# A recommender's interaction and MLP on one core: the first loads without waits, more of the weights turned among chunk 0's products, and chunk 0's grams made whole by three accumulated products

## The chip, the core and the metric

The kernel runs on one core of a Trainium2 chip. Its engines are TensorE (PE; its weight loads, PEld, overlap its products), VectorE (DVE), ScalarE (ACT), GpSimd (POOL) and SyncE (SP), which here issues all DMAs on one queue. Each engine runs its own instructions in order and waits on semaphores for the others. The metric is the device time of one execution in microseconds; the median of several executions is given. All times below are in microseconds unless marked ns.

## What is computed

2048 samples, each with 27 feature vectors of 128 numbers and one more vector of 128 (the bottom MLP's output). For each sample all dot products between its features are made, the 351 below the diagonal are joined to the bottom vector and a zero, and these 480 numbers go through four layers with ReLU and one last product.

```python
dots = jnp.einsum('bfd,bgd->bfg', bottom_output, bottom_output)   # 27 x 27 per sample
pairs = dots[:, _TRIL_I, _TRIL_J]                                 # 351
x = jnp.concatenate([bottom_mlp_output, pairs, pad], axis=1)      # 480
for w, b in ((w0, b0), (w1, b1), (w2, b2), (w3, b3)):             # 1024, 1024, 512, 256
    x = jax.nn.relu(x @ w.T + b)
return x @ w_out.T + b_out
```

## The kernel before

**Numbers in halves.** Products run in a 4-byte form of reduced precision (`F32R`). To keep full precision each operand is split into a high half, which the form holds exactly, and the rest, the low half; a product is then three: high by high, high by low, low by high. ScalarE makes the high half by a copy, VectorE the low one by a subtraction.

**Chunks.** The 2048 samples are 8 chunks of 256. A chunk's products stand with the samples as the 256 moving columns: layer 0 has 8 output tiles of 4 inner tiles, layer 1 has 8 of 8, layer 2 has 4 of 8, layer 3 has 2 of 4, each times three products: 96, 192, 96 and 24. Each output tile (a "slot") fills one of two accumulator banks; ScalarE drains it with ReLU (L654) and VectorE splits it (L772, L774).

**Units.** While chunk c's products run, chunk c+1's features are turned into grams in 16 units of 16 samples. A unit is: a load of 108 rows (4 samples of 27 features) by 4 groups (`load_rows`, L344), 4 transposes (`turn`, L502), a high and a low half (L624, L736), 4 gram products of 256 columns (`gram`, L518), which make high by high and high by low beside each other, 4 copies of the diagonal blocks (`gram_parts`, L641), and on VectorE a transpose of the high by low block and two sums (L751, L753, L763), since low by high is the transpose of high by low. A gram comes `XT_LAG` = 2 units after its turn. The finished grams are spilled to memory (L355) and the pairs gathered from there in another layout (L366); ScalarE and VectorE split the pairs (L664, L806), and the next chunk can begin.

**The written order.** Every engine walks the same list of steps. For chunk c, `chunk_steps` writes the products in order and, after every `HOOK` = 9 of them in layers 0 and 1, one hook: the next unit's steps, or in chunk 0 first the weight groups that are left:

```python
if layer < 2 and done % HOOK == 0:
    hook()
```

**Weights.** They arrive with outputs in the partitions and must be turned. A weight group is 4 transposes of 128 columns (L472, L485), a high half (L609, L610, L613) and a low half (L723, L725, L729); there are 34 and one small one for the biases. GpSimd first puts W0's columns in the kernel's own pair order (L444). Groups can be turned in the head, before chunk 0: eight of W1 between the units of chunk 0, then W0, the small one, W3 and W2; the other eight of W1 are turned in chunk 0's hooks.

**The head.** Chunk 0's own units have no products to hide behind. SyncE issues its 16 feature loads into a ring of 4 buffers, each waiting for the buffer's turn, and weight loads in between:

```python
for u in range(ROWS_RING, 8):
    load_rows(0, u)
load_weights(stage_b[:, 0:2, :], w1, 0, 2, w1_head_loaded[0])
```

Then come the spill and the gather of chunk 0, and its first products. Chunk 7 has no units. The functions that the change touches:

Of the kernel before, what the change touches and what calls it, by code (L numbers as in the profile page):

```python
# [5 lines left out]
F32 = mybir.dt.float32  # L6
F32R = mybir.dt.float32r
ALU = mybir.AluOpType
# [31 lines left out]
W1_HEAD, W0_ALL, SMALL = list(range(9, 17)), list(range(W0_GROUPS)), [W0_GROUPS]  # L40
W1_TAIL, W2_ALL, W3_ALL = list(range(17, 25)), list(range(25, 33)), list(range(33, 35))
ORDER = W1_HEAD + W0_ALL + SMALL + W3_ALL + W2_ALL + W1_TAIL
BETWEEN_UNITS, FIRST_BETWEEN = 8, 7
BEFORE_CHUNK = W_GROUPS - len(W1_TAIL)
W0_TURNED = ORDER.index(W0_ALL[-1]) + 1
assert W0_TURNED >= BETWEEN_UNITS

# [16 lines left out]
HOOK = 9  # L64

OUT_UNIT = 2
# [71 lines left out]
def first_steps():  # L138

    steps = []
    for u in range(UNITS + XT_LAG):
        steps += unit_steps(u)
        if 0 <= u - FIRST_BETWEEN < BETWEEN_UNITS:
            steps.append(("weights", u - FIRST_BETWEEN))
    steps += [("weights", n) for n in range(BETWEEN_UNITS, W0_TURNED)] + [("mlp",)]
    return steps + [("weights", n) for n in range(W0_TURNED, BEFORE_CHUNK)] + [("pairs",)]

def chunk_steps(gram, weights=False):  # L150

    steps, done, unit, group = [], 0, 0, BEFORE_CHUNK if weights else W_GROUPS

    def hook():
        nonlocal unit, group
        if group < W_GROUPS:
            steps.append(("weights", group))
            group += 1  # L160
        elif gram and unit < UNITS + XT_LAG:
            steps.extend(unit_steps(unit))
            unit += 1

    for layer in range(3):
        for m in range(M_TILES[layer]):
            if (layer, m) == (2, 2) and gram:
                steps.append(("mlp",))
            k = 0
            while k < K_TILES[layer]:  # L170
                n = K_TILES[layer] - k
                if layer < 2:
                    n = min(n, (HOOK - done % HOOK) // 3)
                steps.append(("mm", layer, m, k, k + n))
                k += n
                done += 3 * n
                if layer < 2 and done % HOOK == 0:
                    hook()
                if done == OUT_UNIT * HOOK:

                    steps.append(("out",))
    if gram:
        steps.append(("pairs",))
    steps += [("mm", 3, m, k0, k1) for m, k0, k1 in LAST_LAYER]
    return steps

def dlrm_program(nc, x, x_mlp, w0, b0, w1, b1, w2, b2, w3, b3, w_out, b_out, y):
    weights = [w0, w1, w2, w3]
    biases = [b0, b1, b2, b3]  # L190
    with ExitStack() as ctx:
# [6 lines left out]
        def shared(*specs):  # L198

            with ExitStack() as inner:  # L200
# [3 lines left out]
        w_hi = sb("w_hi", [P, TILE0[4] * P], F32R)  # L204
        w_lo = sb("w_lo", [P, TILE0[4] * P], F32R)

        w0_ordered, = shared(("w0_ordered", [P, 8, PAIRS + 1]))
# [4 lines left out]
        stage_pairs, _, stage_dense = shared(("stage_pairs", [P, 8, PAIRS + 1]), ("stage_gap", [P, 3 * 1024 - 8 * (PAIRS + 1)]),  # L216
                                             ("stage_dense", [P, 8, DIM]))
        stage_a, = shared(("stage_a", [P, 4, 1024]))
        h_a = sb("h_a", [P, 8, 2, CHUNK], F32R)

        stage_b, = shared(("stage_b", [P, 4, 1024]))
        h_b = sb("h_b", [P, 8, 2, CHUNK], F32R)
        stage_w3 = sb("stage_w3", [P, 2, 512])

# [9 lines left out]
        stage_small, = shared(("stage_small", [24, P]))  # L235
# [13 lines left out]
        w1_head_loaded = [sem(f"w1_head_loaded{i}") for i in range(2)]  # L249
        w1_tail_loaded = sem("w1_tail_loaded")  # L250
        w2_loaded = [sem(f"w2_loaded{i}") for i in range(2)]
        w3_loaded = sem("w3_loaded")
        rows_loaded = [sem(f"rows_loaded{i}") for i in range(ROWS_RING)]
# [11 lines left out]
        gram_done = sem("gram_done")  # L265
        parts_done = sem("parts_done")
# [22 lines left out]
        x_view = x.rearrange("(c u j s) f d -> c u (s f) j d", u=UNITS, j=UNIT_GROUPS, s=GROUP)  # L289
        mlp_view = x_mlp.rearrange("(c t p) d -> c p t d", t=2, p=P)  # L290
# [25 lines left out]
        def weight_bank(n):  # L316

            if n < BETWEEN_UNITS:
                return acc[:, n % ACC_RING, :]
            return gram_ps[:, n % (GRAM_RING * GRAM_BANKS), :]  # L320

# [16 lines left out]
        def _(sp):  # L338
            def load_rows(d, u):
                if not (isinstance(d, int) and d == 0 and u < ROWS_RING):  # L340

                    sp.wait_ge(turned, d * UNITS + u + 1 - ROWS_RING)
# [3 lines left out]
            def load_weights(dst, w, m0, m1, loaded, k0=0, k1=None):  # L346
                sp.dma_start(dst, w.rearrange("(m p) k -> p m k", p=P)[:, m0:m1, k0:k1]).then_inc(loaded, 16)

            def spill(d):

                sp.wait_ge(grams_done, d * UNITS + UNITS)

# [35 lines left out]
            for u in range(ROWS_RING):  # L389
                load_rows(0, u)  # L390
            load_weights(stage_pairs[:, :, :], w0, 0, 8, w0_loaded, k0=DIM)
            for u in range(ROWS_RING, 8):
                load_rows(0, u)
            load_weights(stage_b[:, 0:2, :], w1, 0, 2, w1_head_loaded[0])
            for u in range(8, 10):
                load_rows(0, u)
            load_weights(stage_b[:, 2:4, :], w1, 2, 4, w1_head_loaded[1])
            load_rows(0, 10)
            load_mlp(0)
            load_rows(0, 11)  # L400
            load_weights(stage_dense[:, :, :], w0, 0, 8, w0_dense_loaded, k1=DIM)
            load_rows(0, 12)
# [6 lines left out]
            load_rows(0, 13)  # L409
            load_weights(stage_w3[:, :, :], w3, 0, 2, w3_loaded)  # L410
            for u in range(14, UNITS):
                load_rows(0, u)

            sp.wait_ge(w0_in_order, 1)
            load_weights(stage_a[:, 0:3, :], w2, 0, 3, w2_loaded[0])

            sp.wait_ge(w_turned, ORDER.index(W1_HEAD[-1]) + 1)
            load_weights(stage_b[:, :, :], w1, 4, 8, w1_tail_loaded)
            spill(0)

            sp.wait_ge(w_turned, W0_TURNED)
            load_weights(stage_a[:, 3:4, :], w2, 3, 4, w2_loaded[1])
            gather(0)
            for u in range(ROWS_RING):
                load_rows(1, u)
            chunk(0)
# [9 lines left out]
        def _(pool):  # L436
# [4 lines left out]

            pool.wait_ge(w0_loaded, 16)
            for col, n, q, step in ROW_RUNS:
                nc.gpsimd.tensor_copy(w0_ordered[:, :, q:q + (n - 1) * step + 1:step], stage_pairs[:, :, col:col + n])  # L444
            nc.gpsimd.tensor_copy(w0_ordered[:, :, PAIRS:], stage_pairs[:, :, PAIRS:]).then_inc(w0_in_order, 1)

            pool.wait_ge(w_turned, W0_TURNED)
            nc.gpsimd.memset(pairs[:], 0.0).then_inc(pairs_zeroed, 1)
# [3 lines left out]
        def _(pe):  # L453
            def turn_weights(n):

                g, bank = ORDER[n], weight_bank(n)
                ring = ACC_RING if n < BETWEEN_UNITS else GRAM_RING * GRAM_BANKS
                if n - ring >= (0 if n < BETWEEN_UNITS else BETWEEN_UNITS):

                    pe.wait_ge(w_done, n + 1 - ring)  # L460
                elif n >= BETWEEN_UNITS:

                    pe.wait_ge(parts_done, UNITS)
                if g < W0_GROUPS:
                    if g == 0:
# [3 lines left out]
                    for k in range(4):  # L469
                        kk = K_LAST if k == 3 else P  # L470
                        src = w0_ordered[:, g, (k - 1) * P:(k - 1) * P + kk] if k else stage_dense[:, g, :]
                        last = nc.tensor.transpose(bank[0:kk, k * P:(k + 1) * P], src, ident[:])  # L472
                elif g == W0_GROUPS:
                    pe.wait_ge(small_loaded, 6 * 16)
                    last = nc.tensor.transpose(bank[:, 0:24], stage_small[0:24, :], ident[0:24, 0:24])
                else:
                    m, part = (g - W0_GROUPS - 1) // 2, (g - W0_GROUPS - 1) % 2
                    src, loaded = [(stage_b[:, m % 4], w1_head_loaded[m % 4 // 2]), (stage_b[:, m % 4], w1_tail_loaded),
                                   (stage_a[:, m % 4], w2_loaded[m % 4 // 3]),
                                   (stage_w3.rearrange("p m k -> p (m k)"), w3_loaded)][m // 4]  # L480
                    if part == 0:
                        pe.wait_ge(loaded, 16)
                    for k in range(4):
                        at = (4 * part + k) * P
                        last = nc.tensor.transpose(bank[:, k * P:(k + 1) * P], src[:, at:at + P], ident[:])  # L485
                last.then_inc(w_turned, 1)

            def turn(d, u):

                r = u % ROWS_RING  # L490
                pe.wait_ge(rows_loaded[r], (d * (UNITS // ROWS_RING) + u // ROWS_RING + 1) * 16)
                if not (isinstance(d, int) and d == 0 and u < TURN_RING):

                    pe.wait_ge(xt_done, d * UNITS + u + 1 - TURN_RING)
# [385 lines left out]
```

## Time and profile before

| | |
|---|---|
| median of 3 runs | 569.57 us (567.98 to 570.96) |
| profiled execution: span, the only time given of it | 570.2 us |
| TensorE, VectorE, ScalarE, GpSimd busy | 95%, 58%, 60%, 2% of the span |
| mean granted TensorE clock | 0.984 of 2.4 GHz |
| moved by DMA | 47.32 MB, mean 83 GB/s |

The profile is of one execution. A number such as L518 is a line of the kernel. In the chain and the timeline several instructions of one line stand in one row, with their number behind an x.

### The profile page before, as it was taken

Reading aid. Unit: us, or ns where it says so; the run is one execution under the profiler, and the core shown is the slowest. Engines: PE = TensorE matmul, PEld = TensorE weight load, DVE = VectorE, ACT = ScalarE, POOL = GpSimd, SP = SyncE. Lnnn points to the kernel's source line nnn. Section 1 sums busy time; section 2 is a strip of 40 time slices with the busy share of each in tenths; the row PEclk is TensorE's granted clock in tenths of the full one; section 3 lists DMA queues with packets and bytes.
Section 4 is the critical chain, followed back from the end, with each engine's and each line's share of the span. In section 5 each row is a group of like instructions: output and inputs, shape, how many; then the busy total and the mean of one; then the engine's idle time right before and its main releaser. Section 6 shows DMA issues by size and latency. Waiting matters only on the chain.

```text
span 570.2 us, 13265 instructions
## 1 busy us (share of the span) xinstructions
PE 542.0 (95%) x4457; PEld 531.7 (93%) x4457; DVE 330.0 (58%) x941; ACT 340.8 (60%) x900; POOL 10.8 (2%) x58
## 2 busy tenths in 40 slices
PE   4768799999999999999999999999999999999997
PEld 3667799999999999999999999999999999999996
DVE  3778678727872488427872488427872488425222
ACT  4988479827971499317971499417981399414112
POOL 1500000000000000000000000000000000000000
PEclk9977899999999999999999999999999999999999
DMA  7987324044304141232304131222304131200000
GB/s 222 260 233 223 89 65 117 12 104 124 109 16 119 37 121 47 61 87 78 109 11 112 43 116 53 62 87 77 109 7 111 47 115 56 55 22 1 1 1 0
DMA packets 89898, 47.32 MB, mean 83 GB/s; under 512 B 25851, under 2 KB 88083, under 8 KB 89875
## 3 DMA queue, kind: packets, MB, share of 16 engines
q1 hardware_dynamic: 89874, 47.02, 29.5%
q8 instruction: 14, 0.23, 0.2%
q14 instruction: 10, 0.07, 0.0%
HBM read 41.03 MB, written 5.98 MB: 82 GB/s over the span
## 4 chain that ended last, share of the span: by engine, by line
PE 73%; ACT 12%; DMA 6%; issue 5%; SPq 2%; DVE 0%; ACTq 0%; DVEq 0%
PE acc L551 61%; ACT parts L641 9%; PE gram_ps L518 6%; PE turned_ps L502 5%; DMA rows<-in_r_bottom_output_dram 5%; ACT xt L624 2%; ACT h_full L654 1%; DMA blocks<-grams 1%; PE gram_ps L485 1%; SPq L366 1%; SPq L355 1%; SPq L344 1%; DMA pairs<-blocks 1%; PE turned_ps L564 0%; PE turned_ps L527 0%
## 5 line engine op out<-in xcount | busy, mean ns | idle before, releaser
L551 PE MATMUL acc<-h_a,w_hi 128*128 128x256 f32 x1152 | 211.2, 283 | 0.9 <-ACT h_full L654 0.8
L654 ACT ACTIVATE h_full<-acc,small_t 128x256 f32<-128x256 f32 x176 | 83.2, 473 | 183.2 <-PE acc L551 181.5
L551 PEld LDWEIGHTS acc<-h_a,w_hi 128*128 128x128 f32 x1152 | 179.2, 191 | 2.2 <-ACT h_full L654 2.2
L641 ACT ACTIVATE parts<-gram_ps 27x216 f32<-27x216 f32 x512 | 173.4, 339 | 5.9 <-PE gram_ps L518 1.1
L551 PE MATMUL acc<-h_a,w_lo 128*128 128x256 f32 x576 | 163.0, 283 | 0.0
L551 PEld LDWEIGHTS acc<-h_a,w_lo 128*128 128x128 f32 x576 | 110.4, 192 | 0.0
L551 PE MATMUL acc<-x,w_hi 128*128 128x256 f32 (+1 forms) x512 | 98.5, 289 | 3.7 <-DVE x L806 3.7
L518 PE MATMUL gram_ps<-xt 128*128 128x256 f32 x512 | 95.9, 312 | 1.0 <-ACT parts L641 0.7
L551 PE MATMUL acc<-h_b,w_hi 128*128 128x256 f32 x512 | 93.3, 284 | 0.0
L736 DVE TENSOR_TENSOR xt<-turned_ps,xt 128x432 fp32r<-128x432 f32 x128 | 77.3, 604 | 18.7 <-ACT xt L624 15.7
L502 PE MATMUL turned_ps<-ident,rows 108*128 108x108 f32 x512 | 72.8, 267 | 16.0 <-DMA rows<-in_r_bottom_output_dram 15.1
L551 PEld LDWEIGHTS acc<-x,w_hi 128*128 128x128 f32 (+1 forms) x512 | 79.9, 192 | 4.9 <-DVE x L806 3.9
L624 ACT ACTIVATE xt<-turned_ps 128x432 fp32r<-128x432 f32 x128 | 67.6, 528 | 24.7 <-PE turned_ps L502 23.6
L551 PEld LDWEIGHTS acc<-h_b,w_hi 128*128 128x128 f32 x512 | 79.7, 192 | 0.0
L518 PEld LDWEIGHTS gram_ps<-xt 128*128 128x128 f32 x512 | 73.2, 201 | 2.3 <-issue 1.3
L502 PEld LDWEIGHTS turned_ps<-ident,rows 108*128 108x128 f32 x512 | 57.4, 146 | 19.0 <-DMA rows<-in_r_bottom_output_dram 13.5
L551 PE MATMUL acc<-x,w_lo 128*128 128x256 f32 (+1 forms) x256 | 72.7, 284 | 0.0
L551 PE MATMUL acc<-h_b,w_lo 128*128 128x256 f32 x256 | 72.4, 283 | 0.0
L772 DVE CAST h_a<-h_full 128x256 fp32r<-128x256 f32 x96 | 28.0, 292 | 75.2 <-ACT h_full L654 74.7
L751 DVE STREAM_TRANSPOSE low_t<-parts 128x128 f32<-128x128 f32 x128 | 39.9, 312 | 44.3 <-ACT parts L641 43.6
L772 DVE CAST h_b<-h_full 128x256 fp32r<-128x256 f32 x64 | 18.8, 294 | 74.3 <-ACT h_full L654 73.9
L551 PEld LDWEIGHTS acc<-x,w_lo 128*128 128x128 f32 (+1 forms) x256 | 49.3, 193 | 0.0
(54 smaller groups left out, 346.3 us busy)
## 6 DMA issues: line engine op xcount, KB each, us to landing
rows<-in_r_bottom_output_dram SPq DMA_DIRECT2D x128, 216.0 KB
blocks<-grams SPq DMA_DIRECT2D x32, 182.2 KB
stage_b<-in_L_rec_w_dram SPq DMA_DIRECT2D x2, 1024.0 KB, 9.6
stage_b<-in_L_rec_w_dram SPq DMA_DIRECT2D x1, 2048.0 KB, 7.8
stage_a<-in_L_rec_w_dram SPq DMA_DIRECT2D x1, 1536.0 KB, 11.5
stage_pairs<-in_L_rec_w_dram SPq DMA_DIRECT2D x1, 1408.0 KB, 9.7
mlp_rows<-r_bottom_mlp_output_dram SPq DMA_DIRECT2D x8, 128.0 KB, 2.2
pairs<-blocks SPq DMA_DIRECT2D x8, 126.0 KB
```

What stands on the lines that cost most here:

```text
L344: sp.dma_start(rows[0:GROUP_ROWS, r], x_view[d, u]).then_inc(rows_loaded[r], 16)
L355: sp.dma_start(blocks[:, :, s * RUN:(s + 1) * RUN], grams[QUAD * s:QUAD * s + FEATS, :, :]).then_inc(spilled, 16)
L366: sp.dma_start(pairs[q % P:q % P + nf * nk, q // P], src).then_inc(gathered, 16)
L502: last = nc.tensor.transpose(turned_ps[:, u % TURN_RING, j * GROUP_ROWS:(j + 1) * GROUP_ROWS], rows[0:GROUP_ROWS, r, j, :], ident[0:GROUP_ ...
L518: last = nc.tensor.matmul(gram_ps[:, u % GRAM_RING * GRAM_BANKS + j // 2, at:at + 2 * P], xt[:, u % XT_RING, j, 0, :], xt[:, u % XT_RING, ...
L551: last = nc.tensor.matmul(acc_slot(slot), weight(wp, layer, m, k), in_tile(layer, k, xp), start=(k == 0 and n == 0), stop=(k == K_TILES[la ...
L624: nc.scalar.activation(xt[:, u % XT_RING, :, 0, :].rearrange("p j (s f) -> p j s f", s=GROUP)[:, :, :, 0:FEATS], turned_ps[:, u % TURN_RIN ...
L641: last = nc.scalar.activation(parts[quad, u % 2, :, :, 0:FEATS], gram_ps[quad, b:b + GRAM_BANKS, :].rearrange("p a (b h n) -> p h (a b) n" ...
L654: nc.scalar.activation(h_full[:, slot % 2, :], acc_slot(slot), ACT.Relu, bias=small_t[:, slot:slot + 1]).then_inc(drained, 1)
L736: nc.vector.tensor_tensor(lo, turned_ps[:, u % TURN_RING, 0:UNIT_COLS].rearrange("p (j s f) -> p j s f", s=GROUP, f=FEATS), hi.bitcast(F32 ...
L751: nc.vector.transpose(low_t[:, u % 2].rearrange("p j g -> p (j g)"), hl.rearrange("p j g -> p (j g)")).then_inc(low_turned, 1)
L772: nc.vector.tensor_copy(high, full).then_inc(high_done, 1)
```

## The change

- **Feature loads of chunk 0.** Eight buffers (`early_rows`, in the memory of `h_b`) are added to the ring of 4; the first 12 loads wait for nothing, the last 4 for a turn. Each moves 112 rows by 4 groups (the turns still read 108). The weight loads between them are gone except W0's; W1's 4 MB follow behind all 16, then the spill, then the first four feature loads of chunk 1, then the gather, then W2 and W3.
- **Weights.** They are loaded into `w_raw`, which has the memory of `w_lo`, and their low halves are written over them ("split in place"). Turned in the head are only W0 and the small group, after the grams. W1's 16 groups, then the 18 unit hooks of chunk 1, then W2's and W3's 10 groups stand in chunk 0's hooks, one after every 6 products (`FIRST_HOOK`). W2's first group waits until `parts_done` counts all 16 units. A slot waits for the weight groups that it reads.
- **Grams of chunk 0.** Per group of 4 samples three products of 128 columns add up in one place: high by high, high by low, low by high (`gram_early`). A unit takes one bank, and the ring has four. Two of its four diagonal blocks are copied to `grams` by ScalarE (`early_move`), two by VectorE (`early_rest`); `gram_parts`, `gram_low` and `gram_sum` are no longer used for chunk 0.
- **GpSimd** clears `pairs` at the start, and no longer after W0 is turned.
- Chunks 1 to 7 are as before.

```diff
-W1_HEAD, W0_ALL, SMALL = list(range(9, 17)), list(range(W0_GROUPS)), [W0_GROUPS]
...
-ORDER = W1_HEAD + W0_ALL + SMALL + W3_ALL + W2_ALL + W1_TAIL
-BETWEEN_UNITS, FIRST_BETWEEN = 8, 7
...
+ORDER = W0_ALL + SMALL + W1_ALL + W2_ALL + W3_ALL
+BEFORE_CHUNK, LATE_WEIGHTS = ORDER.index(W1_ALL[0]), ORDER.index(W2_ALL[0])
...
-HOOK = 9
-
+HOOK, FIRST_HOOK = 9, 6
+FULL_ROWS = 112
+EARLY_SLOTS = 8
+EARLY_BY_ACT = range(2)
...
+def first_hooks():
+    def groups(n0, n1):
+        return [[("weights", n)] for n in range(n0, n1)]
+
+    return groups(BEFORE_CHUNK, LATE_WEIGHTS) + [unit_steps(u) for u in range(UNITS + XT_LAG)] + groups(LATE_WEIGHTS, W_GROUPS)
...
         w_hi = sb("w_hi", [P, TILE0[4] * P], F32R)
+        w_raw, = shared(("w_raw", [P, TILE0[4] * P]))
         w_lo = sb("w_lo", [P, TILE0[4] * P], F32R)
...
+            def load_early(u):
+                if u >= EARLY_SLOTS + ROWS_RING:
+                    sp.wait_ge(turned, u - EARLY_SLOTS - ROWS_RING + 1)
+                sp.dma_start(early_rows_of(u)[0:FULL_ROWS], x_full[0, u]).then_inc(early_loaded[u], 16)
...
+            for u in range(4):
+                load_early(u)
+            sp.dma_start(stage_pairs[:, :, :], w0_rows[:, :, DIM:]).then_inc(w0_loaded, 16)
+            for u in range(4, 8):
+                load_early(u)
+            sp.dma_start(raw_rows(0)[:, :, 0:DIM], w0_rows[:, :, 0:DIM]).then_inc(w0_dense_loaded, 16)
+            load_early(8)
             load_mlp(0)
+            for u in range(9, 12):
+                load_early(u)
...
+            for u in range(12, UNITS):
+                load_early(u)
+            for i in range(4):
+                load_weights(1, w1, 2 * i, 2 * i + 2, w1_loaded[i])
             spill(0)
...
             for u in range(ROWS_RING):
                 load_rows(1, u)
+            gather(0)
+            for i in range(2):
+                load_weights(2, w2, 2 * i, 2 * i + 2, w2_loaded[i])
+            load_weights(3, w3, 0, 2, w3_loaded)
             chunk(0)
...
+            def gram_early(u):
+                pe.wait_ge(xt_done, u + 1)
...
+                ring = GRAM_RING * GRAM_BANKS
+                if u >= ring:
+                    pe.wait_ge(early_moved, u + 1 - ring)
+                    pe.wait_ge(grams_done, u + 1 - ring)
                 for j in range(UNIT_GROUPS):
+                    out, half = gram_ps[:, u % ring, j * P:(j + 1) * P], xt[:, u % XT_RING, j]
+                    for n, (a, b) in enumerate(((0, 0), (0, 1), (1, 0))):
+                        last = nc.tensor.matmul(out, half[:, a, :], half[:, b, :], start=(n == 0), stop=(n == 2))
+                last.then_inc(gram_done, 1)
...
+            def early_move(u):
+                act.wait_ge(gram_done, u + 1)
+                for s in EARLY_BY_ACT:
+                    last = nc.scalar.activation(gram_place(u, s), early_gram(u, s), ACT.Copy)
+                last.then_inc(early_moved, 1)
...
+            def early_rest(u):
+                dve.wait_ge(gram_done, u + 1)
+                for s in range(len(EARLY_BY_ACT), GROUP):
+                    last = nc.vector.tensor_copy(gram_place(u, s), early_gram(u, s))
+                last.then_inc(grams_done, 1)
```

## Rows read from the trace of the kernel before

**Rows 1.** The page: TensorE in 40 slices, and its largest group (mean ns of one).
```profile
PE   4768799999999999999999999999999999999997
PEclk9977899999999999999999999999999999999999
...
L551 PE MATMUL acc<-h_a,w_hi 128*128 128x256 f32 x1152 | 211.2, 283 | 0.9 <-ACT h_full L654 0.8
```

**Rows 2.** The chain that ended last, in order of time, 0 to 75: start, us, what.
```profile
4.01 0.96 PE turned_ps L502 x4
...
29.58 7.63 DMA rows<-in_r_bottom_output_dram
...
46.48 0.35 DVE grams L763
...
46.85 0.96 SPq L355
...
50.53 3.93 DMA blocks<-grams
...
54.48 0.79 SPq L366
...
58.61 2.99 DMA pairs<-blocks
...
62.55 0.97 PE acc L551 x6
```

**Rows 3.** The same chain in chunk 0, and where chunks 1 and 2 begin.
```profile
74.14 0.44 PE gram_ps L485 x4
...
91.76 0.37 PE turned_ps L502 x4
92.14 0.49 PE gram_ps L518 x4
...
132.06 1.10 PE acc L551 x9
...
196.37 1.10 PE acc L551 x9
```

**Rows 4.** Busy time by stretch; the last three columns: granted clock, DMA share, GB/s.
```profile
2.00:4.00 2.00, 0.00 (x0) 0.02 (x1) 0.08 (x1) 0.91 (x1) 0.00 (x0) 1.00 0.69 208
...
4.00:28.00 24.00, 16.02 (x92) 14.63 (x93) 13.87 (x36) 17.33 (x46) 9.34 (x51) 1.00 0.98 262
42.00:47.80 5.80, 3.51 (x16) 2.93 (x15) 3.19 (x12) 4.37 (x13) 0.00 (x0) 0.50 0.88 340
48.20:54.50 6.30, 5.88 (x40) 4.98 (x39) 5.96 (x19) 5.50 (x18) 0.74 (x1) 0.84 0.71 143
```

**Rows 5.** The same view of the two stretches at the lower clock.
```profile
36.60:50.20 13.60, 10.65 (x48) 10.05 (x49) 8.69 (x25) 10.13 (x28) 0.00 (x0) 0.50 0.70 238
...
63.90:67.20 3.30, 3.30 (x18) 3.30 (x17) 1.31 (x3) 1.49 (x3) 0.00 (x0) 0.50 0.33 97
```

**Rows 6.** Timeline of ScalarE in chunk 0: start, us, what.
```profile
92.55 0.53 ACT L624 ACTIVATE xt<-turned_ps 128x432 fp32r<-128x432 f32 x1
...
94.39 0.53 ACT L624 ACTIVATE xt<-turned_ps 128x432 fp32r<-128x432 f32 x1
...
96.23 0.47 ACT L654 ACTIVATE h_full<-acc,small_t 128x256 f32<-128x256 f32 x1
96.61 0.52 ACT L624 ACTIVATE xt<-turned_ps 128x432 fp32r<-128x432 f32 x1
```

**Rows 7.** Timeline of SyncE's queue: gather, then chunk 1's first feature loads.
```profile
54.48 4.90 SPq L366 DMA_DIRECT2D pairs<-blocks  x8
59.42 2.00 SPq L344 DMA_DIRECT2D rows<-in_r_bottom_output_dram  x4
```

**Rows 8.** Timeline of all engines: POOL's reordering, VectorE's halves of ten weight groups.
```profile
12.38 9.24 POOL L444 COPY w_ordered<-stage_pairs 128x8 f32<-128x8 f32 x50 [10.91 <-DMA stage_pairs<-in_L_rec_w_dram]
...
54.15 6.06 DVE L729 TENSOR_TENSOR w_lo<-gram_ps,w_hi 128x512 fp32r<-128x512 f32 x10
```

More of the change, by code:

```diff
@@ L142, in first_steps, with chunk_steps @@
     for u in range(UNITS + XT_LAG):
[L143 to L163, printed above, removed]
+        if u < UNITS:
+            steps.append(("turn", u))
+        if u >= XT_LAG:
+            steps.append(("early", u - XT_LAG))
+    return steps + [("mlp",)] + [("weights", n) for n in range(BEFORE_CHUNK)] + [("pairs",)]
+def first_hooks():
+    def groups(n0, n1):
+        return [[("weights", n)] for n in range(n0, n1)]
+    return groups(BEFORE_CHUNK, LATE_WEIGHTS) + [unit_steps(u) for u in range(UNITS + XT_LAG)] + groups(LATE_WEIGHTS, W_GROUPS)
+def chunk_steps(gram, first=False):
+    steps, done = [], 0
+    hooks = first_hooks() if first else [unit_steps(u) for u in range(UNITS + XT_LAG)] if gram else []
+    every = FIRST_HOOK if first else HOOK
+    hooks.reverse()
     for layer in range(3):
@@ L167, in chunk_steps @@
             if (layer, m) == (2, 2) and gram:
+                assert not hooks
                 steps.append(("mlp",))
@@ L176, in chunk_steps @@
                 done += 3 * n
-                if layer < 2 and done % HOOK == 0:
-                    hook()
-                if done == OUT_UNIT * HOOK:
+                if layer < 2 and done % every == 0 and hooks:
+                    steps.extend(hooks.pop())
+                if done == OUT_UNIT * every:
                     steps.append(("out",))
@@ L468, in turn_weights @@
                         pe.wait_ge(w0_dense_loaded, 16)
[L469 to L475, printed above, removed]
-                else:
[L477 to L480, printed above, removed]
+                else:
+                    row, part = (g - W0_GROUPS - 1) // 2, (g - W0_GROUPS - 1) % 2
+                    if row < 8:
+                        layer, m, loaded = 1, row, w1_loaded[row // 2]
+                    elif row < 12:
+                        layer, m, loaded = 2, row - 8, w2_loaded[(row - 8) // 2]
+                    else:
+                        layer, m, part, loaded = 3, g - W3_ALL[0], 0, w3_loaded
@@ L481, in turn_weights @@
                     if part == 0:
                         pe.wait_ge(loaded, 16)
-                    for k in range(4):
-                        at = (4 * part + k) * P
-                        last = nc.tensor.transpose(bank[:, k * P:(k + 1) * P], src[:, at:at + P], ident[:])
-                last.then_inc(w_turned, 1)
+                src = raw_rows(layer)[:, m, :]
+                for k in range(4):
+                    kk = K_LAST if layer == 0 and k == 3 else P
+                    at = (4 * part + k) * P
+                    last = nc.tensor.transpose(bank[0:kk, k * P:(k + 1) * P], src[:, at:at + kk], ident[:])
@@ L497, in turn @@
+                if u == 0:
                     pe.wait_ge(mlp_done, d)
@@ L585, in _ @@
                 if step[0] == "turn":
-                    turn(0, step[1])
-                elif step[0] == "gram":
-                    gram(0, step[1])
+                    turn_early(step[1])
+                elif step[0] == "early":
+                    gram_early(step[1])
                 elif step[0] == "weights":
```

191 lines of the change are left out of this document (98 added, 93 removed).

## The prediction

> **What bounds the kernel now.** I read the page first: TensorE is busy in nine tenths or more of nearly every slice from the fifth on, and the thin part is the head, four slices of 14.3 us [rows 1]. The chain of waits in order of time shows what the head waits for [rows 2]: loads of feature rows, then ScalarE's copies of the gram blocks, then the spill of the grams, then the gather of the pairs; the first product that needs pairs starts at 62.55. After it the chain is TensorE alone. The tenth product of chunk 1 starts at 132.06 and that of chunk 2 at 196.37 [rows 3]; from 132.06 on nothing is edited, so the whole change is worth what it does to that 132.06. It splits into 62.55 of head and 69.51 of chunk 0.
>
> **The head, before.** The last feature load lands at about 37.2, the last gram is summed at 46.83, and then a fixed tail follows: 46.85 to 54.47 for the spill (7.6 us) and 54.48 to 61.60 for the gather (7.1 us), 0.95 us for splitting the pairs [rows 2]. The DMA engines were full nearly all of 4 to 28 (share 0.98, 262 GB/s), so deleting waits on SyncE creates no bandwidth; it only changes what comes first [rows 4]. In that time three big weight loads cut in between the feature loads; the new order puts all 16 feature loads ahead of W1.
>
> **The head, after, step by step.**
> Loads: 16 feature loads of 224 KB are 3.67 MB, W0 2.0 MB and the MLP rows 0.13 MB: 5.8 MB. At the 262 GB/s of 4 to 28 that is 22 us, at the 340 GB/s of 42 to 47.8, when only big weight packets moved, 17 us [rows 4]. I take 20.6 us (280 GB/s, nearer the first, since three fifths of the bytes are feature rows), from a start at about 2: the last feature row is there at 22.6 (19 to 24) in place of 37.2. W1 follows, 4.19 MB at 340 GB/s, 12.3 us: it ends at 35 (31 to 37).
> The loads grow from 108 to 112 partitions. The four first loads moved at only 208 GB/s with a DMA share of 0.69 [rows 4], as if a quarter of the engines stood idle. The Trainium skill's page "DMA: Bandwidth & Descriptors", section "Why a DMA increments its semaphore by 16 and not by 1", says that a hardware DMA uses the largest number of engines up to 16 that divides its outermost dimension: 12 for 108 partitions, 16 for 112. The row agrees with it; by it the sixteen loads would end some 2 us sooner, inside my bounds.
> TensorE: a turn is 4 transposes, 0.37 us at full clock, and 0.96 for the first ones, cold [rows 2, 3]. A gram was 4 products of 256 columns, 0.49 us, so 0.12 each; it becomes 12 of 128 columns. No row has a product of this type with 128 columns. Bound from below: half of 0.12, 0.06 each. Nearest row: the weight transposes, 128 columns of 4-byte data, 0.44 us for 4, 0.11 each [rows 3]. Bound from above: the 0.283 that one product lasts from end to end if the three that add to one place don't overlap [rows 1]. I take 0.107 (0.11 less the gap at the group's edge). A unit is then 0.37 + 12 x 0.107 = 1.65 us at full clock, twice that at half. Sixteen units are 26.4. Two turns are done before the first gram can start, so dense work begins at 6.3; if the clock stays at 1.2 GHz for about 4.7 us more (after the first product at 62.55 the clock was full for good from 67.2 on, 4.7 us later [rows 2, 5]) the stage loses 2.35. End: 6.3 + 26.4 - 0.7 + 2.35 = 34.4, and 0.6 for the last moves: 35.0 in place of 46.85.
> ScalarE and VectorE are under this: ScalarE drops from 1.84 us a unit (one copy of 0.53 and four of the gram, the rest [rows 6]) to the 0.53 and two copies no longer than the old ones, at most 1.2; VectorE exchanges three steps for two small copies.
> Spill: the issue at 35.0 lands 7.6 later, 42.6. The queue must be free too: W1 ends at 35, and the four spills moved their data in about 5.9 us of 48.2 to 54.5 [rows 4], so the queue's own bound is 40.9. The grams decide by 1.7 us; W1 stands right behind them, and this is where an even earlier gram end would be lost.
> Gather: four feature loads for chunk 1 now go ahead of it. Their issue (2.0 us) fits in the spill's flight, 39.5 to 41.5, and their transfer (about 3.9) overlaps the gather's own 4.9 us of issue [rows 7]. I count nothing; if they delay it, up to 2 us. W2 and W3 are issued behind the gather and are wanted 50 us later. So: 42.6 + 7.1 + 0.95 = 50.7 in place of 62.55, a gain of 11.9 us. POOL's reordering of W0 (12.4 to 21.6 before) is over when the grams end; the 8 W0 groups follow them, at some 0.6 us each by the pace of VectorE's copies [rows 8], and lie inside 35 to 50.7. If that cover were gone they would cost those 5 us.
>
> **Chunk 0, after.** Before: 69.51 us with 8 weight groups among the products.
> Weights: 26 groups stand there now. A group costs TensorE 0.44 [rows 3], 18 more are 7.9 us. Before, these 18 were turned while TensorE waited for loads, the spill and the gather, where they cost nothing. VectorE's part, the longer one (6.06 us for ten [rows 8]), plus half a slot's split, at most as much again, comes to a little under a hook of 6 x 0.12 + 0.44 = 1.16 us, so nothing more is lost there.
> Units: their hooks come every 6 products and no longer every 9. TensorE's own work in one is 0.72 + 0.37 + 0.49 = 1.58 us. ScalarE needs 1.84 a unit [rows 6] and 0.38 for a drain every 24 products, 0.09 a hook: 1.93. Before it was 1.94 against 1.98, and TensorE hid it. ScalarE becomes the bound of this stage. From the first turn to the last copy it takes 0.4 of latency, 1.2 of starting idle, 16 x 1.84 and 1.6 of drains, 32.6 us; the next step on TensorE, the first W2 group, waits for that last copy. TensorE alone would need 18 x 0.72 + 16 x 0.86 = 26.7. Stall: 5.9 us (4 to 7).
> Clock: before, 63.9 to 67.2 ran at the half clock [rows 5], worth 1.7. The wait before the first product is longer now, and the half clock can hold from the first product to 4.7 us after it, worth up to 2.4. I take 2.1: 0.4 more.
> Chunk 0: 69.5 + 7.9 + 5.9 + 0.4 = 83.7, 14.2 longer.
>
> **Sum.** 50.7 + 83.7 = 134.4 in place of 132.06: 2.3 us later. The profiled execution's span is 570.2, 0.7 above the median of the three runs, 569.57; its own time is not given apart from the span. So 572.5 for such a span, 571.9 as a median: 572.0. This is within 0.5% (2.85 us), which is about what a measurement of this kernel can tell from no change.
>
> The skill's page "TensorE: Matmul & The Clock Gate", section "Back-to-back issue gap", gives 81 ns for a sustained weight load and product with 128 columns. No row here shows that. By it a unit is 1.3 us, the grams end near 30, the queue's 40.9 decides and the result is 1.7 us lower.
>
> **Rivals.**
> A, slower: the narrow products lose their one-pass rate. A product of 256 columns runs at about one column per cycle (0.12 us at 2.4 GHz) while the transposes of 4-byte data already take two cycles a column (0.11 for 128) [rows 3], so the rate depends on the form. Against it: the same type runs everywhere else at full rate; for it: in every row it has 256 columns. With four cycles a column a product is 0.213, a unit 2.93, 16 units 46.9, and the grams end at 6.3 + 46.9 - 0.7 + 2.35 + 0.6 = 55.4. Spill, gather and split add 15.7: 71.1, and with 83.7 the mark is 154.8, 22.7 later: 592. At 0.283 each it would be 604. From 0.107 on each further 0.01 costs 12 x 16 x 0.01 = 1.9 us, so it takes the result over 0.5% from 0.11. The page "FP8 and Floating Point Precision", section "TensorE Precision Notes", tells of four passes for true fp32; that is the mechanism which this rival would need, and no run here shows it for this type.
> B, faster: the narrow products cost 0.06, the even 16-engine loads bring W1's end to 31, and TensorE's queue absorbs part of ScalarE's lag. Spilled at 37, first product at 45.1, stall 4: 45.1 + 81.8 = 126.9, 5.2 earlier: 564.5.
> C, the removed waits give nothing, because the one queue is full anyway and the spill stands behind W1 and slower mixed packets: W1 ends at 38, spill at 44, four feature loads hold the gather 2 us: first product at 54. Mark 137.7, 5.6 later: 575.
>
> **How the numbers follow.** The forecast's case (567 to 575) has 0.45, A 0.35 (586 to 597), B 0.12, C 0.08. The forecast's own case puts 0.31 within 0.5%, 0.11 slower, 0.03 faster. So faster 0.15, within 0.5% 0.32, slower 0.53; the likeliest single case still is the near tie at 572. The range must reach into A: from 566.5 to 595; the forecast's own range is 567 to 575.
>
> **What would show it.** The last feature load near 23 and the last gram near 35; a narrow product's pitch near 0.107 (A: over 0.2; B: 0.06); W1 landed near 35; first product of x with pairs near 50.7; in chunk 0, 26 weight groups, unit hooks of 1.93 us with TensorE idle before turns or grams for ScalarE's parts; the same 64.3 us for chunk 1. The forecast is wrong if the narrow product isn't near 0.107, if ScalarE's lag is hidden, or if the spill doesn't start when the grams end.

## The result, and the profile after

The changed kernel takes 599.26 us (median of 4 runs, 598.27 to 599.88), the kernel before 570.27 in the same comparison: 1.051 times the time, 95% interval 1.047 to 1.054. It is 29 us slower.

The page of the changed kernel: its span, then TensorE, granted clock and DMA in 40 slices of 14.9 us.

```profile
span 596.1 us, 13538 instructions
...
PE   6999399989999999999999999999999999999997
...
PEclk9999789999999999999999999999999999999999
DMA  9930633313130313122231314041412232210000
```

The DMA engines are full for two slices, partly busy in the third and idle in the fourth, while TensorE works on at nine tenths: the loads are done early, as intended, and the head no longer waits for them. (Before the first recorded change of the clock, at 60.9 us here, the page shows full clock whatever it was.) The chain that ended last, in order of time, from 0 to 80 (start, us, what), which answers to [rows 2]:

```profile
6.88 0.98 PE turned_ps L531 x4
7.86 2.49 PE gram_ps L571 x12
10.35 0.74 PE turned_ps L531 x4
11.09 2.49 PE gram_ps L571 x12
...
49.81 7.62 PE gram_ps L571 x36
...
57.81 0.35 ACT grams L695
...
58.23 0.96 SPq L399
...
65.97 0.79 SPq L410
...
70.07 2.86 DMA pairs<-blocks
...
73.88 1.01 PE acc L619 x3
```

From 6.88 to the last gram TensorE alternates without a pause between four turns of 0.74 us and twelve narrow products of 2.49. That is 3.23 us a unit, 51.6 for the sixteen. The two last copies end at 58.15 (46.83 before), and the spill, the gather and the split follow as they did. The first product that needs pairs starts at 73.88 (62.55 before). The chain's row at the tenth product of chunk 1, which answers to the last two of [rows 3]:

```profile
157.81 1.09 PE acc L619 x9
```

So the mark moved from 132.06 to 157.81: 11.3 us in the head and 14.4 in chunk 0. From there to the end the two kernels take 438.3 and 438.1 us.

Busy time by stretch (columns as in [rows 4]): the units of the head, the half clock around chunk 0's start, and the unit hooks in chunk 0.

```profile
3.80:57.50 53.70, 52.32 (x258) 51.87 (x258) 20.15 (x47) 18.97 (x47) 8.89 (x51) 1.00 0.63 178
...
67.80:77.80 10.00, 3.92 (x18) 3.92 (x19) 2.02 (x5) 2.10 (x5) 0.00 (x0) 0.50 0.81 272
...
94.80:127.60 32.80, 29.31 (x237) 27.17 (x235) 24.39 (x71) 30.25 (x84) 0.00 (x0) 1.00 0.28 82
```

In the last row ScalarE is busy 30.25 of 32.8 us and TensorE 29.31, while in the kernel before TensorE was busy for all of 77 to 109 and ScalarE for 29.49 of these 32 us. TensorE's waits from 94 to 129 (line waited for, us in total, times, longest):

```profile
PE gram_ps L526 <- ACT parts L710: 1.3, 1, 1.3
PE gram_ps L586 <- ACT parts L710: 1.2, 2, 0.8
PE turned_ps L531 <- DVE xt L806: 0.8, 2, 0.4
```

The first is the first W2 group waiting for the copies of unit 15. Waits that the view shows come to 3.3 us. The rest of the loss seems to be in short gaps that busy time hides: the 237 products and transposes in 29.31 us are 0.124 each, and 282 of nearly the same mix in the kernel before, in 32.0 us, are 0.113.

**The medians and the spans.** Every profiled execution of the changed kernel and of its variants is 2.4 to 3.5 us longer than its span. The kernel before, run again as the last experiment, takes 568.8 us with a span of 566.3, the same 2.5. If the same holds for the execution that the prediction was read from, with a span of 570.2, it was one of the longer ones; its head was 4.1 us later than that of the second profile. Against the second profile the head moved by 15.4 and chunk 0 by 14.4, together the 29.8 by which the spans differ; the medians differ by 29.0.

### The profile page after: what moved, and what is told of

Same layout as the page of the kernel before. It is cut to its first block, busy times and chain, and to the rows that moved or that the text cites. A ratio compares the mean times of both kernels' runs of the same rounds, so it can differ in the third digit from the quotient of the medians.

```text
span 596.1 us, 13538 instructions
## 1 busy us (share of the span) xinstructions
PE 572.0 (96%) x4585; PEld 562.4 (94%) x4585; DVE 328.9 (55%) x925; ACT 332.6 (56%) x868; POOL 10.3 (2%) x58
## 4 chain that ended last, share of the span: by engine, by line
PE 75%; ACT 15%; issue 6%; SPq 2%; DMA 1%; ACTq 0%; DVE 0%
PE acc L619 56%; ACT parts L710 11%; PE gram_ps L571 7%; PE turned_ps L531 6%; PE gram_ps L586 4%; PE gram_ps L526 2%; ACT xt L689 2%; ACT h_full L726 1%; DMA early_rows<-in_r_bottom_output_dram 1%; SPq L399 1%; SPq L410 1%; SPq L385 1%; DMA pairs<-blocks 0%; PE turned_ps L632 0%; PE turned_ps L595 0%
## 5 line engine op out<-in xcount | busy, mean ns | idle before, releaser
L710 ACT ACTIVATE parts<-gram_ps 27x216 f32<-27x216 f32 x448 | 152.0, 339 | 4.3
L586 PE MATMUL gram_ps<-xt 128*128 128x256 f32 x448 | 80.3, 301 | 1.4 <-ACT parts L710 1.2
L531 PE MATMUL turned_ps<-ident,rows 108*128 108x108 f32 x464 | 63.9, 260 | 1.0 <-DVE xt L806 0.8
L586 PEld LDWEIGHTS gram_ps<-xt 128*128 128x128 f32 x448 | 60.4, 190 | 4.1 <-issue 2.1
L826 DVE STREAM_TRANSPOSE low_t<-parts 128x128 f32<-128x128 f32 x112 | 34.9, 312 | 37.3 <-ACT parts L710 36.6
L531 PEld LDWEIGHTS turned_ps<-ident,rows 108*128 108x128 f32 x464 | 50.5, 143 | 2.4 <-issue 2.4
```

Source lines behind the costliest of these rows:

```text
L531: last = nc.tensor.transpose(turned_ps[:, u % TURN_RING, j * GROUP_ROWS:(j + 1) * GROUP_ROWS], src[0:GROUP_ROWS, j, :], ident[0:GROUP_ROWS ...
L586: last = nc.tensor.matmul(gram_ps[:, u % GRAM_RING * GRAM_BANKS + j // 2, at:at + 2 * P], xt[:, u % XT_RING, j, 0], xt[:, u % XT_RING, j]. ...
L710: last = nc.scalar.activation(parts[quad, u % 2, :, :, 0:FEATS], gram_ps[quad, b:b + GRAM_BANKS, :].rearrange("p a (b h n) -> p h (a b) n" ...
L826: nc.vector.transpose(low_t[:, u % 2].rearrange("p j g -> p (j g)"), hl.rearrange("p j g -> p (j g)")).then_inc(low_turned, 1)
```

## The experiments

Two theories stood after the result, beside the plain one that the loads or the weights were to blame. In the first, a narrow product costs what the prediction took, two cycles a column, but TensorE's clock isn't raised while such products fill it. In the second, it costs four cycles a column, the prediction's rival A. At half and full clock respectively, both give 0.213 us.

| run | edit against the changed kernel | median us | ratio to before, 95% | first product with pairs | chunk 1 begins |
|---|---|---|---|---|---|
| the change | | 599.26 | 1.051 (1.047 to 1.054) | 73.88 | 156.09 |
| e1 | grams of chunk 0 as before | 581.44 | 1.020 (1.016 to 1.025) | 56.85 | 138.92 |
| e2 | narrow products repeated to 256 columns | 578.66 | 1.015 (1.010 to 1.019) | 54.85 | 137.44 |
| e3 | (in the kernel before) narrow grams alone | 589.68 | 1.034 (1.030 to 1.039) | 79.94 | 146.21 |
| e4 | 144 extra products at full clock | 602.96 (one run) | | | |
| e5 | 40 wide products before the first turn | 579.08 | 1.015 (1.013 to 1.017) | 54.30 | 135.94 |
| e6 | e2, W1 turned in the head, hooks of 9 | 567.51 | 0.997 (0.995 to 0.998) | 55.80 | 124.79 |
| e7 | W1 turned in the head, hooks of 9 | 588.09 | 1.031 (1.028 to 1.033) | 77.00 | 147.52 |
| e8 | W1 turned in the head, hooks of 6 | 593.86 | 1.041 (1.039 to 1.044) | 77.18 | 151.54 |
| e9 | 24 wide products first, W1 turned in the head, hooks of 9, eight feature loads first | 564.83 | 0.992 (0.990 to 0.994) | 53.25 | 122.24 |
| e10 | e9 with 108-row loads | 565.97 | 0.993 (0.991 to 0.995) | 53.40 | 123.92 |
| e11 | the kernel before, again | 569.69 | 1.000 (0.998 to 1.002) | 58.45 | 126.25 |

The last two columns are from each run's one profile. "Chunk 1 begins" is its first product, 1.7 us ahead of the prediction's mark.

**e1, the grams of before in the changed kernel.** `first_steps` uses `unit_steps` for chunk 0, and every engine runs `gram`, `gram_parts`, `gram_low`, `gram_sum` for it:

```diff
-        if u < UNITS:
-            steps.append(("turn", u))
-        if u >= XT_LAG:
-            steps.append(("early", u - XT_LAG))
+        steps += unit_steps(u)
```

> The changed kernel with chunk 0's grams made as before the change: 4 products of 256 columns a unit, ScalarE's four copies, VectorE's transpose and two sums; loads, weights and hooks stay changed. Theory 1 (the narrow products cost about two cycles a column, 0.107 at 2.4 GHz, but while they fill TensorE its clock stays at 1.2 GHz): the clock rises within the first 20 us, ScalarE's 1.84 a unit decides, the grams end near 36 in place of 58, the first product that needs pairs is near 52 in place of 73.9, chunk 0 stays 83.9 long: some 22 us faster than the changed kernel, about 577. Theory 2 (a narrow product costs four cycles a column at any clock, and the clock had been full): the same head, so this run alone doesn't tell them apart, but the turns would last 0.74 here too. Rival (the early loads or the weights are what made the head late): it stays above 590.

The chain that ended last:

```profile
3.32 10.00 DMA early_rows<-in_r_bottom_output_dram
...
40.77 0.96 SPq L394
...
56.85 1.01 PE acc L612 x3
```

17.8 us faster than the changed kernel, 17.0 of it in the head. It is still slower than before, though its head is earlier than that of e11 by 1.6 us. The first row is new: from 3.32 to 13.36 the chain is a feature load, the fifth one, which stands behind W0's pair columns. Behind it ScalarE sets the pace, as expected, and so the grams end at 40.7 and not at 36.

**e2, the same number of products, twice as wide.**

```diff
-                        last = nc.tensor.matmul(out, half[:, a, :], half[:, b, :], start=(n == 0), stop=(n == 2))
+                        last = nc.tensor.matmul(out, half[:, a, :], half[:, b:b + 1, :].broadcast_to([P, 2, P]),
+                                                start=(n == 0), stop=(n == 2))
```

> The changed kernel with each of the 12 gram products of a unit widened from 128 to 256 columns, by moving the same half twice; the result's left half is copied as before. Twice the columns, the same number of products and weight loads. Theory 1: with the wide form the clock rises; a product is 0.12 at full clock, a unit 0.37 + 12 x 0.12 = 1.84, the grams end near 38, the first product with pairs near 54: about 20 us faster than the changed kernel though it does twice the columns. If the number of products or of weight loads keeps the clock down, a unit costs 0.74 + 12 x 0.213 = 3.3 as now and nothing changes. If a wide product is full rate but the clock is low for another reason, the same 3.3.

The chain that ended last:

```profile
3.32 9.63 DMA early_rows<-in_r_bottom_output_dram
...
12.99 0.59 PE turned_ps L532 x4
13.58 1.45 PE gram_ps L573 x12
...
31.81 1.45 PE gram_ps L573 x12
...
38.77 0.96 SPq L400
...
54.85 1.01 PE acc L622 x3
```

Twelve products of 256 columns take 1.45 us where twelve of 128 took 2.49, and the turns before them 0.37. The recorded clock rose at 12.1 us. The kernel moves twice the columns and is 20.6 us faster. So neither the number of products nor that of weight loads kept the clock down. The loads and the weights are as in the changed kernel, so they did not make its head late either. (The wider results leave a ring of two units in place of four, which can only hold this run back.)

**e3, the narrow grams alone, in the kernel before.** `gram_early`, `early_move` and `early_rest` go into it as the change has them, for chunk 0's steps only; all else stays.

> The kernel before with one part of the change alone: chunk 0's grams by three accumulated products of 128 columns and four small copies; loads, ring of 4, weight groups between the units and hooks of 9 as before. Theory 1: TensorE needs 3.23 a unit at the half clock, 52 us for 16 units, and 0.85 for each of the 8 weight groups among them unless those raise the clock: grams end at 56 to 63 in place of 46.8, chunk 0 as before, 69.5: 9 to 16 us slower than before. Rival (the narrow products cost nothing beside the late loads; the change's loads and weights made it slow): no difference from before.

The chain that ended last:

```profile
7.20 2.49 PE gram_ps L530 x12
9.68 0.74 PE turned_ps L516 x4
...
51.17 0.72 PE turned_ps L516 x4
...
54.38 0.87 PE acc L499 x4
...
64.39 0.96 SPq L368
```

The unit costs 3.23 us here too, and the weight groups between the units 0.87, the price at half clock, so they don't raise it among these products either. The clock rose at 68.7, after the last gram and 4.3 us into W0's groups. 20 us slower than before against my 9 to 16: the spill was issued at 64.4 where I had at most 63, and the usual start of it is 43.1 (e11), not 46.85.

**e4, the price at full clock.** After W0's groups, on TensorE only:

```diff
+            pair = xt[:, XT_RING - 1, 0]
+            for n in range(48):
+                nc.tensor.matmul(acc[:, 1, 0:2 * P], pair[:, 0, :], pair.rearrange("p h n -> p (h n)"), start=True, stop=True)
+            for n in range(96):
+                nc.tensor.matmul(acc[:, 1, 0:P], pair[:, 0, :], pair[:, 0, :], start=True, stop=True)
```

> The changed kernel with 48 extra products of 256 columns and then 96 extra ones of 128 columns put on TensorE after W0 is turned, while it waits for the spill and the gather; their results are not used. The clock was full from 60.9 on there. Theory 1: the wide ones take 0.11 to 0.12 each and the narrow ones start at 0.107 (two cycles a column at 2.4 GHz); within the 96 the clock falls and they become 0.213. Theory 2: the narrow ones take 0.213 from the first one and the clock stays full. A third case: 0.107 to the end, and the clock stays full, so narrow products keep a clock that is already up but don't raise it. One column a cycle would be 0.055.

The timeline of TensorE (start, us, what), and busy time by stretch:

```profile
54.73 2.33 PE L571 MATMUL gram_ps<-xt 128*128 128x128 f32 x10
...
63.90 6.02 PE L663 MATMUL acc<-xt 128*128 128x256 f32 x48
69.76 10.83 PE L665 MATMUL acc<-xt 128*128 128x128 f32 x96
80.43 0.45 PE L619 MATMUL acc<-x,w_hi 128*128 128x256 f32 x2
```

```profile
61.60:80.00 18.40, 18.21 (x158) 17.66 (x156) 5.12 (x16) 3.94 (x14) 0.00 (x0) 1.00 0.76 243
```

The narrow ones start at 69.76 and the next product at 80.43: 10.67 us for 96, 0.111 each. The wide ones need 5.86 for 48, 0.122. So at 2.4 GHz a product of 128 columns costs nine tenths of one of 256: counted by columns, about two cycles each against one. Both forms have one weight load a product, and no run separates a price per column from a fixed time per product. The clock stays at 1.00 to the end. Theory 2 is out, and the third case that I had written down is what happened: narrow products keep a clock that is up and don't raise one that is down.

**e5, the clock raised first.** `x0`'s part is cleared by VectorE, its result is unused:

```diff
             pe.wait_ge(ident_ready, 2)
+            pe.wait_ge(warm_ready, 1)
+            for n in range(40):
+                nc.tensor.matmul(acc[:, 1, 0:2 * P], x0[:, 1, 0, 0:P], x0[:, 1, 0, :], start=True, stop=True)
             for step in first_steps():
```

> The changed kernel with one addition: 40 products of 256 columns on a cleared operand, whose result is not used, from about 2 us on, before the first turn. The narrow products stay as they are. Theory (wide products raise the clock, narrow ones don't raise it but keep it when it is up): the clock rises by about 10, four turns last 0.37 and twelve narrow products 1.3 from then on, a unit 1.65 to 1.7, grams end near 38 in place of 58, first product with pairs near 54: about 19 us faster than the changed kernel, 580, although 8 us of work were added. If the price of a narrow product in the head is bound by something else (its operands just written, four banks), the turns speed up and the narrow ones stay at 0.2: only about 6 us faster. If narrow products let the clock fall when loads interrupt them, something between.

The chain that ended last, and busy time by stretch:

```profile
16.20 1.31 PE gram_ps L572 x12
17.51 0.39 PE turned_ps L532 x4
...
31.53 1.31 PE gram_ps L572 x12
...
37.61 0.35 ACT grams L699
...
54.30 1.01 PE acc L620 x3
```

```profile
6.20:47.00 40.80, 35.63 (x316) 33.75 (x314) 26.72 (x66) 24.90 (x66) 8.84 (x51) 1.00 0.88 246
```

The clock rose at 6.1 and held for 41 us of mainly narrow products; a unit is 0.39 + 1.31 = 1.70. The forty added products take 6.83 us, the first turn starts at 8.80, and the kernel is 20 us faster. The loads, the grams and the weights are those of the changed kernel, so the low clock is shown to be the cause of the late head. This is the change with only the failed assumption repaired: its head is 4.2 us earlier than e11's, and the kernel is still 1.5% slower than before. The rest is chunk 0.

**e6, e7, e8: what chunk 0 pays.** W1 is turned in the head, after W0. Two constants:

```diff
-HOOK, FIRST_HOOK = 9, 6
+HOOK, FIRST_HOOK = 9, 9
-BEFORE_CHUNK, LATE_WEIGHTS = ORDER.index(W1_ALL[0]), ORDER.index(W2_ALL[0])
+BEFORE_CHUNK, LATE_WEIGHTS = ORDER.index(W2_ALL[0]), ORDER.index(W2_ALL[0])
```

e7 is this, e8 the second line alone, e6 both with e2's edit.

> The changed kernel with two edits: the gram products widened to 256 columns by repetition, as in the second experiment, and W1's 16 groups turned in the head after W0, while TensorE waits for the spill and the gather, so that only the 18 unit hooks and 10 groups stay in chunk 0, one after every 9 products. My reading: the head stays at 54.9 (16 groups of 0.6 fit nearly whole between 45 and 55; up to 2 us over), chunk 0 costs 69.5 + 2 x 0.44 = 70.4 in place of 83.9: mark at 126 to 128 where before had 132.06, so 4 to 6 us faster than before, 564. If chunk 0's extra 14.4 us came from elsewhere, it stays above before, near 578.

> The changed kernel with W1's 16 groups turned in the head and hooks of 9 in chunk 0; narrow grams and the cold clock stay. Chunk 0 would be 70.4 in place of 83.9, the head up to 1.5 later than 73.9: 12 to 13.5 us faster than the changed kernel, near 586.5. If TensorE's extra time in chunk 0 was not the 18 groups and the stall for ScalarE, less.

> As the run with W1 in the head, but a hook after every 6 products as in the changed kernel. It separates the two terms of chunk 0: against that run only the stall for ScalarE's copies comes back, 5.9 us (4 to 7); against the changed kernel only the 16 groups are gone, 7.0 us. If the stall is hidden, both runs are equal.

The chain of e6:

```profile
45.63 9.78 DVE w_lo L804 x16
...
55.80 0.98 PE acc L622 x6
```

The stretch of e7 at the half clock:

```profile
77.10:80.30 3.20, 3.20 (x16) 3.20 (x17) 0.85 (x3) 0.75 (x2) 0.00 (x0) 0.50 1.02 389
```

Chunk 0, from the first product with pairs to chunk 1, is 82.2 us in the changed kernel, 70.5 in e7, 74.4 in e8, 69.0 in e6 and 67.8 before. e7 pays a half clock at its start, which e8 doesn't, worth 1.6; so the hooks of 6 cost 3.8 + 1.6 = 5.4 us, where 5.9 was forecast, and the medians differ by 5.8. From e8 to the changed kernel it is 7.9 us. The changed kernel runs at the half clock from its first product to 77.9, worth 2.0, which leaves 5.9 for the 16 groups, where 7.0 was forecast. e7 is 2.7 us longer than before with the half clock in both; its two more groups are 0.9 of that, and the other 1.8, in a chunk whose unit hooks now come first, is not traced. So the two causes named in the prediction are there, each to about 1 us, and this third part makes up for the shortfall.

e7 came 11.2 us ahead of the changed kernel, short of the 12 to 13.5 expected: its head is 3.1 us later and not 1.5, mainly since VectorE's halves of W1's sixteen groups stand ahead of the pairs. e6's first row shows the same halves, 9.78 us. They end at 55.41; the pairs' first high half was ready at 54.67, so they cost about 0.7 there. e6 beats before by 0.3%; my 564 was 3.5 us too good, since I took the first profile of before for a typical one.

**e9 and e10, put together.** e7, with narrow grams, 24 wide products first, and the feature loads 4 to 7 moved ahead of W0's pair columns:

```diff
-            sp.dma_start(stage_pairs[:, :, :], w0_rows[:, :, DIM:]).then_inc(w0_loaded, 16)
             for u in range(4, 8):
                 load_early(u)
+            sp.dma_start(stage_pairs[:, :, :], w0_rows[:, :, DIM:]).then_inc(w0_loaded, 16)
```

> What the runs so far point to, put together: the changed kernel's loads and narrow grams, 24 wide products on a cleared operand before the first turn, W1 turned in the head, hooks of 9, and eight feature loads instead of four ahead of W0's pair columns. The runs before it showed rows 4 on landing only at 13, behind W0's columns, with TensorE idle. Now loads 4 to 7 land by 9, units of 1.70 run from about 7 on, the sixteen end near 33 in place of 38.7. The spill then stands behind W1 in the one queue (W1 landed at 37, four spills 5.9 us): spilled at 43, first product with pairs at 52 in place of 55.8. So 3 to 4 us faster than the run with W1 in the head and repeated products: span near 561, median near 564. If the queue doesn't hold the spill, up to 6 us faster; if POOL's later reordering of W0 delays W0's groups and with them W1's, nothing is gained.

The chain of e9:

```profile
1.96 5.06 PE acc L655 x24
7.03 0.39 PE turned_ps L532 x4
...
9.31 1.31 PE gram_ps L572 x12
...
35.83 0.35 ACT grams L699
...
43.08 9.78 DVE w_lo L805 x16
...
53.25 0.98 PE acc L620 x6
```

The gap before the fifth load is gone, the grams end at 36.2, and VectorE's halves of the weights are again what the pairs' split waits behind, for about 0.7 us. 0.8% faster than before. The grams came 2.5 us earlier than in e6, not the 5.7 that I expected. The first turn starts at 7.03, as expected; but sixteen units of 1.70 from there already end at 34.2, and the chain has another 1.3 of waiting for the first halves and 0.7 of last copies, which I had left out.

e10 sets `FULL_ROWS = 108`.

> The same kernel with chunk 0's feature loads at 108 rows in place of 112. If 108 rows go over 12 engines and 112 over 16, the sixteen loads move 36 packets an engine in place of 28, some 2 to 3 us more in total, W1 and the spill come that much later: 2 us slower. If the loads are spread evenly either way, 4% fewer bytes and no difference.

It is 1.1 us slower, and the intervals overlap. Busy time by stretch in e9 and then in e10, the same 3.2 us:

```profile
54.70:57.90 3.20, 3.20 (x31) 3.20 (x30) 2.37 (x6) 2.15 (x5) 0.00 (x0) 1.00 1.03 392
```

```profile
54.70:57.90 3.20, 3.20 (x18) 3.20 (x17) 1.32 (x3) 1.45 (x3) 0.00 (x0) 0.50 1.02 400
```

e10's profile fell to the half clock there and e9's didn't, which is worth 1.6 of the 1.7 us between the two marks, and their spills were issued at 36.26 and 36.41. The wider loads do move faster: from 2 to 4, when only feature loads are under way, e9 has a DMA share of 0.89 and 261 GB/s, e10 0.75 and 218. But this gained nothing that shows in the head. The medians' 1.1 us go with the clock: three executions of e9 have a mean clock of 0.998 and take 564.3 to 564.4 us, its other three have 0.996 or 0.997 and take 565.3 to 566.3, and all six of e10 have 0.996 or 0.997 and take 565.4 to 566.6. Whether the loads have a part in which of the two comes stays open.

**e11, the kernel before again.**

> The kernel before, unchanged, run like an experiment, to read the time that its executions take outside the span. Every run of the changed kernel and of its variants was about 2.5 us longer than its span. If the same holds here, the span of an ordinary execution is about 567.5 and the first profile was of a slow one; if it is near nothing, the changed kernel adds about 2.5 us outside the profiled span.

The chain's row at the first product with pairs:

```profile
58.45 1.65 PE acc L551 x6
```

The first case: 568.8 with a span of 566.3, and a head that ends at 58.45, 4.1 us ahead of [rows 2]. Chunk 0 is 67.8 long in both.

## Why the prediction was wrong

The forecast was a near tie at 572.0; the kernel takes 599.3. The step that failed is the one in the head: "if the clock stays at 1.2 GHz for about 4.7 us more ... the stage loses 2.35". The clock stayed at 1.2 GHz for the whole stage. The 4.7 us came from chunk 0, where TensorE runs wide products; I carried it over to a stage that is filled with a form no row showed. The sixteen units took 51.6 us instead of 26.4 + 2.35, and the grams ended at 58.15 instead of 35.0. That the clock is the cause is shown by e5: the same narrow products, with the clock up before them, end their grams at 37.96. The signs that the prediction named did not include the clock.

- **A narrow product's price, 0.107:** right at full clock, 0.111 in e4 and 0.109 in e5; 0.2075 by the chain at half.
- **Rival A** had nearly the time (592, mark 154.8 against 157.8) and the wrong mechanism. Four cycles a column would have made a warm start useless; e4 and e5 rule it out. That its time came near is luck: the cost per product doubled, as it said, but by the clock. (At 0.283 each its sum gives 605, not 604.) The four passes of true fp32 (Trainium skill, "FP8 and Floating Point Precision", "TensorE Precision Notes") have no part in this.
- **The Trainium skill's 81 ns** for a weight load and product of 128 columns (Trainium skill, "TensorE: Matmul & The Clock Gate", "Back-to-back issue gap"): not seen for this type; 109 to 111 ns.
- **The loads:** done early, and no limit in the changed kernel once the third unit is there at 6.84. W1 was there at about 35, as forecast: the DMA share is 1.04 from 32 to 34 and 0.02 from 36 on. The reading of [rows 4], that 108 rows leave a quarter of the engines idle, fits e10 (0.75). But I missed the gap that e1 and e2 show, up to 13.4, and took the feature loads as a steady stream from 2 us on. At full clock it would have made the forecast's own head later: with e5's prices behind e2's gap, 12.99 + 0.59 + 11 x 0.39 + 14 x 1.31 + 0.7 puts the end of the grams at 36.9 in place of 35.0, an estimate. e5 itself has its first product at 54.3, where the sum had 50.7, mainly because its added products hold the first turn back to 8.80.
- **Spill and gather:** 58.23 to 73.88 is 15.65 us, as before. The queue behind W1 was no limit, since the grams came so late; the four feature loads ahead of the gather cost nothing there, and up to about 0.6 us in e5 (16.3 from the spill's issue to the product).
- **Chunk 0:** 14.2 longer by the sum, 14.4 measured, in part by luck: the stall for ScalarE is 5.9 by the sum and 5.4 by e7 and e8, the 16 groups 7.0 and 5.9, and 1.8 us that the sum does not have make up for it. Chunk 1 takes the same 64.3 us, as forecast.
- **The chances:** slower had 0.53. The case nearest in time, A, had 0.35; a clock that stays low through the whole stage was no case and had no chance of its own. The range ended at 595.

## What to carry to other kernels

A price per instruction is not enough for a stage that TensorE fills: ask too whether the form that fills it was seen to raise the clock, and when no row shows it, put the half clock on the whole stage as a case of its own. A few wide products of no use ahead of such a stage can pay: 6.8 us of them made e5 20 us faster than the changed kernel. Work that moves out of a wait into a stage that is bound by TensorE costs nearly its full time there. Hooks set closer together can make the next busiest engine, here ScalarE, the one that bounds. Count both against what the head is to gain.

## What the runs showed of the hardware

- In this 4-byte form (F32R) a product of 128 columns takes nearly as long as one of 256, 0.111 against 0.122 us at 2.4 GHz (e4). Whether columns or something fixed per product set this isn't shown.
- 50 us of narrow products with turns between them, without a pause, left the clock at 1.2 GHz in the changed kernel, and so they did in e3 with eight weight groups among them. The weight transposes that followed had 2.4 GHz 2.6 us after they began, 4.3 us in e3. With wide products it rose at 12.1 (e2) and 6.1 (e5, whose operands for them are all zeros). Once at 2.4 GHz, the narrow products kept it for 10.7 us (e4, unbroken) and in a stretch of 41 us (e5). What in the narrow form fails to raise the clock isn't shown: the weight transposes also have 128 columns and take as long, 0.11 us [rows 3].
- The whole of a profiled execution was 2.4 to 3.5 us longer than its span, before (e11) and after.
